# Residue one-hots by broadcast and low parts on ScalarE in the dense turns of a graph network, with two loads issued sooner

## What is computed

```python
h = relu(layernorm(x))
msg = edge_weight[:, None] * (h[dst] @ W_i + h[src] @ W_j + edge_attr @ W_e)
x = x + segment_sum(msg, dst) + h @ W_self          # layer 0
h = relu(layernorm(x))
def sage(h, W_l, b, W_r):
    mean = segment_sum(h[src], dst) / max(count(dst), 1)[:, None]
    return mean @ W_l.T + b + h @ W_r.T
h = relu(sage(h, W1_l, b1, W1_r))
x = x + log_softmax(sage(h, W2_l, b2, W2_r))        # layer 1, two steps
```

## Time and profile before

| | |
|---|---|
| median of 3 runs | 1,671.7 us (1,670.32 to 1,675.69) |
| profiled execution | 1,664.25 us, span 1,662.4 us |
| mean granted TensorE clock | 0.933 of full |
| TensorE busy | 1,418.8 us, 85% of the span |
| VectorE busy | 979.4 us, 59% |
| ScalarE busy | 600.4 us, 36% |
| GpSimd busy | 727.2 us, 44% |
| DMA | 441.26 MB, mean 265 GB/s |

### The profile page before, as it was taken

The page is one execution under the profiler, slowest core; times in us unless marked ns, Lnnn a source line. Parts: engine busy times, 40 slices in busy tenths (PEclk is TensorE's granted clock), DMA queues, the critical chain, the costliest instruction groups (busy, mean ns, idle before and its releaser), DMA issues. The chain is left out here.

```text
span 1662.4 us, 25953 instructions
## 1 busy us (share of the span) xinstructions
PE 1418.8 (85%) x8448; PEld 1013.4 (61%) x8449; DVE 979.4 (59%) x4423; ACT 600.4 (36%) x1479; POOL 727.2 (44%) x783
## 2 busy tenths in 40 slices
PE   2587778898897887978898867799999979999997
PEld 0465556666675665766666546466666656666664
DVE  7799999889897987988897848200101030010204
ACT  5366656555646446465542325200000010020203
POOL 8777765667776766677677748000000000000000
PEclk9699889999998898999999988899999989999999
DMA  8467777988988978888799872577767657777773
GB/s 267 150 219 275 274 250 257 323 283 302 307 285 275 315 254 291 284 301 296 259 321 292 263 240 88 225 281 271 295 263 302 262 202 274 278 303 269 309 273 138
DMA packets 178853, 441.26 MB, mean 265 GB/s; under 512 B 24619, under 2 KB 104924, under 8 KB 175388
## 3 DMA queue, kind: packets, MB, share of 16 engines
q1 hardware_dynamic: 155996, 391.75, 65.3%
q0 software_dynamic: 22432, 46.97, 10.3%
q10 hardware_dynamic: 288, 0.85, 0.1%
HBM read 318.94 MB, written 120.55 MB: 264 GB/s over the span
## 5 line engine op out<-in xcount | busy, mean ns | idle before, releaser
L629 POOL DMA_INDIRECT home<-h_table,src_i x676 | 654.2, 968 | 280.3 <-issue 198.7
L1119 PE MATMUL psAE<-home 128*128 128x350 f16 x3528 | 541.3, 314 | 13.4 <-issue 8.7
L1119 PEld LDWEIGHTS psAE<-home 128*128 128x128 f16 x3528 | 339.1, 96 | 210.5 <-issue 12.6
L1029 PE MATMUL psAE<-home 128*128 128x256 f32 x1352 | 331.6, 406 | 44.1 <-DMA home<-h_table,src_i 20.1
L1029 PEld LDWEIGHTS psAE<-home 128*128 128x128 f32 x1352 | 274.0, 205 | 100.9 <-issue 54.7
L1477 DVE TENSOR_SCALAR home<-iota_h,dst_rel,home 128x128 f32<-128x128 f16 x832 | 222.6, 364 | 30.3 <-PE psAE L1029 27.8
L788 ACT ACTIVATE home<-psW 128x490 f16<-128x490 f32 x418 | 211.3, 577 | 59.1 <-PE psW L1038 47.4
L1419 DVE TENSOR_SCALAR home<-iota_h,tile 128x245 f16<-128x245 f16 x1004 | 208.9, 301 | 30.1 <-PE psW L1048 16.4
L1423 DVE TENSOR_SCALAR home<-iota_h,tile 128x128 f16<-128x128 f16 x1004 | 179.3, 281 | 0.0
L1581 DVE SCALAR_TENSOR_TENSOR home<-psAE,home 128x350 f32<-128x350 f32 x18 | 9.4, 523 | 253.6 <-PE psAE L1119 253.6
L1038 PE MATMUL psW<-home 128*128 128x245 f16 x836 | 127.8, 285 | 36.1 <-DVE home L1423 33.8
(11 more groups left out here) (211 smaller groups left out, 1173.6 us busy)
## 6 DMA issues: line engine op xcount, KB each, us to landing
home<-counts SPq DMA_DIRECT2D x36, 4287.5 KB, 13.7
counts<-home SPq DMA_DIRECT2D x126, 612.5 KB
home<-edges SPq DMA_DIRECT2D x64, 845.0 KB
weighted<-home SPq DMA_DIRECT2D x24, 1225.0 KB, 6.8
home<-weighted SPq DMA_DIRECT2D x36, 800.0 KB
home<-h_table,src_i POOLq DMA_INDIRECT x676
home<-h_table SPq DMA_DIRECT2D x36, 256.0 KB
home<-inv_row SPq DMA_DIRECT2D x36, 175.0 KB, 13.5
```

The costliest lines, as they stand in the source:

```text
L629: pool.indirect_dma_start(out=rows[to][:, j, :], out_offset=None, in_=from_table[:, :], in_offset=bass.IndirectOffsetOnAxis(ap=src_i[b][:, ...
L1029: done = nc.tensor.matmul(psA[:, 0:2 * P].rearrange("p (n f) -> p n f", n=2), onehot[:, j, :], both_of(s, b, j), start=(j == 0), stop=(j = ...
L1119: last = nc.tensor.matmul((psA, psE)[r][:, 0:SNODES].rearrange("p (c d) -> p c d", c=SUPER), halves[:, a, n, :], tiles[:, :, a, :], start= ...
```

## The change

In a dense turn the 20 residue one-hots are made by one VectorE tensor_tensor for each part (8 and 12 groups), both operands broadcast over a shape of partitions x groups x 128. Where a part crosses a tile of edge records there are two; with these sizes none does. The keys stay as they are, and so do plain turns. The low parts are made on ScalarE as the high ones, by an ACTIVATE with the column of low weights as its scale, right behind the high one of the same group. `low_hots` and the semaphore `whot_low` are gone. After the loop, SyncE issues the read-back of the weight rows ahead of the own rows, with its wait for the node rows, and the second set of counts of pass one ahead of the wait for the reciprocals, with its wait for the last first-layer product.

```diff
@@ sync, after the loop @@
+                for b in range(2):
+                    sp.wait_ge(node_out[b], 16 * (CHUNKS // 2 - b))
+                sp.dma_start(node_weight_rows, node_rows[0, 0:USED].rearrange("(t p) -> t p", p=P)).then_inc(weight_in, 16)
                 sp.wait_ge(own_out, 16 * BLOCKS)
                 sp.wait_ge(piece_done, DSUPERS * PIECES)
                 for n, (lo, hi) in enumerate(OWN_PARTS):
                     columns = slice(lo * UNROLL * FEATS, hi * UNROLL * FEATS)
                     sp.dma_start(accN[:, columns], own_rows[:, columns]).then_inc(own_back[n], 16)
-                for b in range(2):
-                    sp.wait_ge(node_out[b], 16 * (CHUNKS // 2 - b))
-                sp.dma_start(node_weight_rows, node_rows[0, 0:USED].rearrange("(t p) -> t p", p=P)).then_inc(weight_in, 16)
...
                 load_counts(1, 0)
+                sp.wait_ge(mixed[0], BLOCKS)
+                load_counts(1, 1)
                 sp.wait_ge(inv_made, 2)
                 sp.dma_start(inv_row.rearrange("(p n) -> p n", p=LINES), deg_lines).then_inc(inv_out, 16)
                 sp.wait_ge(inv_out, 16)
                 for p in PASSES:
                     if p == 1:
-                        sp.wait_ge(mixed[0], BLOCKS)
                         load_inverse(1, 0)
-                        load_counts(1, 1)
                         load_inverse(1, 1)
@@ scalar, weigh_hots @@
-                    done = nc.scalar.activation(whot_all[k % 2][:, j, 0, :], ghot(4 * k + j)[1], ACT.Copy, scale=w_parts[t][:, 0, at:at + 1])
+                    for n in range(2):
+                        done = nc.scalar.activation(whot_all[k % 2][:, j, n, :], ghot(4 * k + j)[1], ACT.Copy, scale=w_parts[t][:, n, at:at + 1])
@@ tensor, weigh_pair @@
                 pe.wait_ge(whot_ready, ORDER[i] * 5 + k + 1)
-                pe.wait_ge(whot_low, ORDER[i] * 5 + k + 1)
@@ vector, count_groups @@
-                    for k in ks:
-                        last = nc.vector.tensor_scalar(ghot(k)[1], iota_h[:, 0:P], record_of(k, 2), None, ALU.is_equal)
+                    if c < DENSE:
+
+                        for t, at, k, n in tile_parts(c):
+                            lo, hi = max(k, ks[0]), min(k + n, ks[-1] + 1)
+                            if lo < hi:
+                                shape = [P, hi - lo, P]
+                                last = nc.vector.tensor_tensor(ghots[:, lo:hi, GCOLS + 1:GW], iota_h[:, 0:P].unsqueeze(1).to_broadcast(shape),
+                                                               tile_of(t)[:, 2, at + lo - k:at + hi - k].unsqueeze(2).to_broadcast(shape), ALU.is_equal)
+                    else:
+                        for k in ks:
+                            last = nc.vector.tensor_scalar(ghot(k)[1], iota_h[:, 0:P], record_of(k, 2), None, ALU.is_equal)
...
-                        if i and ORDER[i - 1] < DENSE:
-                            low_hots(i - 1, (4,))
...
-            def low_hots(i, ks):
-
-                c = ORDER[i]
-                for k in ks:
-                    if c * 5 + k >= 2:
-                        dve.wait_ge(made, slot_end(i, "W", k - 2) if k >= 2 else slot_end(WHEN[c - 1], "W", k + 3))
-                    for j in range(4):
-                        t, at = divmod(c * GROUPS + 4 * k + j, P)
-                        last = nc.vector.tensor_scalar(whot_all[k % 2][:, j, 1, :], iota_h[:, 0:P], tile_of(t)[:, 2, at:at + 1],
-                                                       w_parts[t][:, 1, at:at + 1], ALU.is_equal, ALU.mult)
-                    last.then_inc(whot_low, 1)
...
-                if c < DENSE:
-                    low_hots(i, (0, 1))
...
-                if c < DENSE:
-                    low_hots(i, (2, 3))
```

More of the change, by code:

```diff
@@ L219, in gnn_program @@
         ghot_all = carve(hT, in_hT, GROUPS * GW // 2, f16)
+        ghots = ghot_all.rearrange("p (k w) -> p k w", k=GROUPS)
         own_hot = carve(hT, in_hT, NCHUNK // 2, f16)
@@ L238, in gnn_program @@
         own_hT = carve(accN, in_N, P)
+        assert in_N[0] <= USED
         node_weight_rows = accN[0:BLOCKS, USED:USED + P]
@@ L325, in gnn_program @@
         made, kept = sem("made"), sem("kept")
-        whot_ready, whot_low = sem("whot_ready"), sem("whot_low")
+        whot_ready = sem("whot_ready")
         w_out = [sem(f"w_out{h}") for h in range(2)]
```

## The result

The changed kernel takes 1,689.92 us (median of 10 runs, 1,678.15 to 1,696.44), the kernel before in the same comparison 1,674.61 us (10 runs): a ratio of 1.0097, 95% interval 1.0072 to 1.0122, 1.0% slower. Forecast were 1,680.5 us and a range of 1,665 to 1,695. The profiled execution took 1,689.24 us, close to its median; that of before lies 10 us under its median, so some 10 us of the difference between the two traces is not the change's.

What follows compares the result with a forecast made beforehand. ScalarE's scaling, W4 and VectorE's second part bind dense turns. Loop +23.7, weight rows -5.8, second counts load -7.7 and -1.4 make +8.8 us on 1,671.7, so 1,680.5 us; range 1,665 to 1,695.

Steps and rivals of the forecast that it cites:

- What binds: Dense turns of the loop: the chain of ScalarE's scaling, W4 and VectorE's second part binds, in all 12.
- W4: Last of a dense turn's five weighted pairs on TensorE; forecast 17.7 us after the first scaling in general.
- W1: Second of the five weighted pairs, ahead of the sum; forecast 6.5 us past the fifth turn's first scaling.
- The walk of a dense turn: Fifth dense turn followed through ScalarE's queue: W4 starts 3.1 us late; same working for all twelve sums to 23.7 us.
- the last group's 1.17 us a turn: Four more scalings in each dense turn's last group on ScalarE: 1.17 us a turn, 14 us in 12.
- The term of 23.7 us for the loop: Lateness of W4 summed over the 12 dense turns: 23.7 us slower, bounds 14 and 41.
- rival 3: Dense turns: TensorE's longer waits lower its clock, slowing the sum matmuls, 12 x 2.0 = 24 us; chance 0.10.
- VectorE's relief at nothing: Loop: the 57.5 + 5 us taken off VectorE gains nothing, being covered by its wait for W4.
- The signs named as wrong: Loop: W4 released by something else, VectorE's saving shortening the turn behind a dense one, or plain turns changing.
- The broadcast: Residue one-hots of a dense turn on VectorE: 2.98 us instead of 3.42, winning 0.44 us a turn.
- Weight rows: After the loop: weight rows sent first let GpSimd's products start 5.8 us sooner; bounds 5 and 6.5.
- Second counts load: Pass one after the loop: earlier load removes TensorE's stall, 7.7 us, and the slow start behind it, 1.4 us.

Runs made afterwards that it cites:

- second and first experiment: Second: kernel before with the low parts on ScalarE, ratio 1.0175. First: kernel before with the two loads after the loop moved, ratio 0.9913.
- the reordering: Changed kernel with the last group's scaling on ScalarE ahead of the third weighted pair's eviction, same work: ratio 0.9975.
- the three buffers: Changed kernel with a third buffer for the scaled one-hots, so ScalarE scales groups earlier: ratio 0.999.

## Why the prediction was right, and where its numbers were off

- *What binds.* Right for the end of the turn: ScalarE's scaling, W4 and VectorE's second part bind in all 12 dense turns; the low parts returned to VectorE restore both the waits and the time, and an order of ScalarE's queue changes the time with the work unchanged. Ahead of the sum ScalarE sets W1 (6.66 us behind the first scaling) in six turns, the first five and the eleventh; in the other six TensorE itself is later, 7.5 to 11.4 us. So not every added instruction counts. Of the 70 us that ScalarE does more, 35.6 came out in these turns: the last group's 14.0 in full; of the 28 for groups 0 and 1, ahead of the sum, 14.0, and 3.1 of these by TensorE's clock; of the 28 for groups 2 and 3, which ScalarE makes while the sum runs, the fifth turn's 0.6, the rest of that stretch being slower sums.
- *The walk of a dense turn.* Right to 0.2 us at W1, the copy and W4 in the fifth turn, for which it was made, and the last group's 1.17 us a turn is there in full (14.0 us). Carried over to the other turns it did less well: first scaling to W4 grew by 4.5, 3.1, 4.5 and 6.1 us in the first four (1.6, 1.6, 2.7 and 3.4 forecast), and in the ninth it shrank by 1.2, where 1.2 more was forecast. In part the misses cancel in the sum. ScalarE's idle time between first and last scaling was to be gone; it fell from 55 to 21 us over the 12 turns and is gone in the fifth alone. The loop was to end near 1,006 us; the first load behind it is issued at 1,023.90.
- *The term of 23.7 us for the loop* was too small. By the traces it is 39.8, by the measured ratio 16.2 + 15.2 = 31.4; the gap between them is about what the profiled execution of before was quick by (10 us). Against the kernel that differs from the changed one in ScalarE's edit alone it is 28.6 us by the ends of the loop (1,007.57 and 978.99) and 35 by the ratios. What was missing of the 23.7: I took rival 3 as one that happens everywhere or not at all. It happens in five of 12 turns, and with 0.6 us of ScalarE's queue in the fifth it makes the +7.7 us between sum and copy, 5.0 of which came back in the first four sums when TensorE was kept busy. Not all of it is the change's: the trace of before has no sum over 5.85 us in these turns, but with the low parts on VectorE such sums come too, 6.44 and 6.99 us in the first and fourth turn of the kernel without the ScalarE edit. Over 5.78 us each, the 12 sums took 7.0 us more in the changed kernel and 1.9 in that one; 6.4 and 1.4 in the second and first experiment; but 3.6 and 3.4 when those two were run again. Ahead of the sum the forecast had 23.7 - 14.0 = 9.7 us, and 14.0 were measured: 4.3 more. There the walk went by ScalarE's durations and let TensorE's pairs take 1.00 us, while W1 took 1.82 in the first four turns: by the start of the sum (8.3 against 7.5 us) that is 3.1 of the 4.3. The remaining 4 of 39.8 lie outside these stretches.
- *VectorE's relief at nothing.* Right at the pace that the prediction was made for: VectorE's wait for W4 grew from 2.4 to 7.6 us in the fifth turn, and plain turns kept their length (502.6 and 505.7 us in sum). Dense turns, measured on VectorE, became shorter (166.3 to 139.1), as it hurries through them, and those behind them longer by more (251.9 to 317.2): I had written that both would grow by 1 to 3 us. A turn cut on an engine that is not the bound says only where it waits. The signs named as wrong (another releaser of W4, a shorter turn behind a dense one, a change in plain turns) did not come. No run takes the low parts off VectorE without giving them to ScalarE, so that this relief is worth nothing is read from the waits, not shown by a run. At the other pace a relief of VectorE ahead of the first scaling does pay: the broadcast's 1.4 to 1.7%.
- *The broadcast.* 2.96 us against 2.98. The Trainium skill ("VectorE: DVE Perf Modes", section on the TRN2 errata) has a formula for a float32 tensor_tensor, (N + 151)/0.96 ns, which gives an estimate of 1.22 and 1.76 us; the trace agrees (1.216 and 1.744).
- *Weight rows.* -6.15 us against -5.8, but by another road: I had the first own part bind. It landed in 4.9 us; the products started at 1,030.50 behind the turning of the weights, and TensorE had turned those only after its last sum, at 1,029.92. That is so in all five kernels with this tail at this pace: the products start 2.2 to 2.4 us behind the end of the last sum, where before it was 8.8. So the price was near by luck: it rests on a last sum that happened to end about when the first own part landed, and in two of the five (the reordering and the three buffers) the last sum came 4 us later, and the products with it.
- *Second counts load.* -7.6 and -1.4 us against -7.7 and -1.4.

## What to carry to other kernels

Before moving work from the engine with the larger busy share, find which wait ends last in the stage, and walk that stage by the receiving engine's queue; if it is that engine's instruction that releases the last wait, each one added behind the last gap counts in full, even at 53% busy, and those ahead of a gap only by what the gap doesn't take (here 35.6 of 70 us came out). Then add what a longer wait does to TensorE's clock in the matmuls behind it: here about a fifth of the loss in the loop by one pair of traces, and next to nothing by another. Walk more than one turn, as the one that comes out clean is not the mean. And look at the order of the queue that binds: here one scaling moved ahead of one eviction was worth about 1% (0.7% to 1.2%), with no work taken out.

## What the runs showed of the hardware that was not expected

A gather on GpSimd takes longer while VectorE runs a broadcast. GpSimd's timeline of the changed kernel, then VectorE's in the same stretch:

```profile
157.31 0.94 POOL L631 DMA_INDIRECT home<-h_table,src_i  x1 [0.30 <-issue]
158.55 2.48 POOL L631 DMA_INDIRECT home<-h_table,src_i  x1 [0.30 <-issue]
161.34 0.99 POOL L631 DMA_INDIRECT home<-h_table,src_i  x1 [0.30 <-issue]
```

```profile
158.47 1.74 DVE L1430 TENSOR_TENSOR home<-iota_h,home 128x1536 f16<-128x1536 f16 x1
```

Of 676 gathers 28 take over 1.2 us (5 before), and 21 of these lie over a broadcast; the mean is 1,009 ns against 968. In every kernel with the broadcast it is 992 to 1,012 ns, in every one without it 958 to 968, whatever ScalarE does. It cost nothing that the runs show: the broadcast alone made the kernel faster, and GpSimd waits 89.7 us for free buffers. The Trainium skill ("GPSIMD Engine Reference", Specifications) says that GpSimd shares its interfaces to SBUF (the on-chip memory that holds the operands) with VectorE and contends with its instructions that have two SBUF inputs; the rows fit it, though no run here tells this cause from another.

The other surprise is the chip itself: the same kernel takes 2,050 us on two chips and 1,675 to 1,682 elsewhere, with gaps of 0.45 to 1.03 us between VectorE instructions that wait for nothing visible, and an edit that spares instructions (the broadcast) was worth 1.4% there, where at the other pace about 4 us (0.2%) were left for it, within the interval.
